# Last attention pair: where the embedding average and the first experts' preparation stand in the instruction order

## The reference

```python
h = tok(x)                                # patches @ W + b + pos, class token in front
h = concatenate([h, txt], axis=1)         # 178 tokens
h = h + attn(layernorm(h))
h = h + ffn(layernorm(h))

# attn: 12 heads, causal
xn  = layernorm(x, ln_w)
avg = mean(wte, axis=0)                   # wte is 50257 x 192
Q   = xn * W_qk[head]
a   = softmax(causal(Q @ Q.T / sqrt(192)))
out = a @ (xn - avg)                      # per head
out = out / [1 .. S]                      # per row
out = concat(heads) @ W_o.T

# ffn: 16 routed experts and a shared one, hidden size 128
s = softmax(x @ gate_w + gate_b)          # 4 of 8 groups, then 4 of 16 experts, weights times 2.5
y = sum over experts of w * (silu(x @ Wu + bu) * (x @ Wg + bg)) @ Wd + w @ bd
y = y + shared expert
```

## Time and profile before

| what | value |
|---|---|
| median of 3 runs | 476.73 us (476.62 to 477.12) |
| profiled execution, its own time | 476.07 us |
| its span | 474.2 us |
| PE busy | 448.3 us (95%) |
| DVE busy | 279.2 us (59%) |
| ACT busy | 181.8 us (38%) |
| mean granted TensorE clock | 0.977 of full |

### The profile page before, as it was taken

One profiled execution on the slowest core, in us unless ns is written; L12 is line 12 of the kernel. 1 busy time (PEld: TensorE's weight loads), 2 busy tenths in 40 slices (PEclk: granted clock), 3 DMA queues, 4 the chain that ended last, 5 costly groups with the idle time before them and its releaser, 6 DMA issues. The chain is left out here.

```text
span 474.2 us, 7663 instructions
## 1 busy us (share of the span) xinstructions
PE 448.3 (95%) x2836; PEld 403.3 (85%) x2836; DVE 279.2 (59%) x789; ACT 181.8 (38%) x581; POOL 97.5 (21%) x110
## 2 busy tenths in 40 slices
PE   8699999999999999982998999989999999999997
PEld 7488779877898778972866999989999999999996
DVE  4488866476654976304497635697447654754443
ACT  1467566256644376411445035532312232121211
POOL 3012122221122211210013015921180027000000
PEclk9799999999999999996799999999999999999999
DMA  8968999999999999978316022322323222222220
GB/s 208 252 242 155 212 214 213 213 214 214 213 213 215 212 214 214 212 138 200 133 38 238 1 74 67 64 47 65 86 63 64 63 85 59 60 73 72 75 65 25
DMA packets 23686, 65.01 MB, mean 137 GB/s; under 512 B 2876, under 2 KB 13332, under 8 KB 23266
## 3 DMA queue, kind: packets, MB, share of 16 engines
q0 software_dynamic: 7904, 40.86, 41.1%
q1 hardware_dynamic: 14882, 22.68, 17.9%
q10 hardware_dynamic: 864, 1.00, 0.7%
HBM read 61.88 MB, written 1.27 MB: 133 GB/s over the span
## 5 line engine op out<-in xcount | busy, mean ns | idle before, releaser
L805 PE MATMUL bank<-woT,area_o 128*128 128x192 f32 (+1 forms) x432 | 71.9, 327 | 0.0
L520 ACT ACTIVATE pm<-bank,nmax 128x128 f32<-128x128 f32 x96 | 34.5, 369 | 96.2 <-DVE nmax L1024 96.2
L1110 DVE TENSOR_TENSOR area_b<-area_b,area_w 128x356 f32<-128x356 f32 x64 | 33.9, 529 | 62.7 <-ACT area_b L585 62.6
L805 PEld LDWEIGHTS bank<-woT,area_o 128*128 128x128 f32 (+1 forms) x432 | 69.8, 182 | 0.6 <-issue 0.6
L422 POOL DMA_DIRECT2D area_w<-in_L_attn_wte_dram x26 | 31.4, 1226 | 127.7 <-DMA area_w<-in_L_attn_wte_dram 127.7
L887 PE MATMUL bank<-area_w_r,area_o_r 128*128 128x356 f32 x112 | 43.9, 392 | 0.0
L585 ACT ACTIVATE area_b<-bank,area_k 128x356 f32<-128x356 f32 x32 | 17.8, 558 | 58.9 <-PE bank L891 58.9
L754 PE MATMUL bank<-pT,xn 128*128 128x356 f32 x96 | 39.7, 495 | 0.0
L543 ACT ACTIVATE area_b<-xb,w 64x192 f32<-64x192 f32 x96 | 38.3, 447 | 0.8
L923 PE MATMUL bank<-area_k,area_b 128*128 128x192 f32 (+1 forms) x192 | 36.8, 327 | 0.0
L888 PE MATMUL bank<-area_w_r,area_o_r 128*128 128x356 f32 x112 | 36.4, 325 | 0.0
(11 more groups left out here) (218 smaller groups left out, 1019.4 us busy)
## 6 DMA issues: line engine op xcount, KB each, us to landing
area_w<-in_L_attn_wte_dram POOLq DMA_DIRECT2D x28, 1344.0 KB, 12.6
area_w<-gate_rows SPq DMA_DIRECT2D x64, 178.0 KB, 3.0
area_k<-in_experts_dram SPq DMA_DIRECT2D x8, 353.0 KB, 6.5
area_a<-in_experts_dram SPq DMA_DIRECT2D x6, 353.0 KB, 5.1
woT<-in_L_attn_W_o_dram SPq DMA_DIRECT2D x1, 1728.0 KB, 15.9
area_o<-in_x_dram SPq DMA_DIRECT2D x4, 384.0 KB, 9.1
area_w<-area_w POOLq DMA_DIRECT2D x1, 1344.0 KB, 9.8
area_b<-in_experts_dram SPq DMA_DIRECT2D x3, 353.0 KB, 6.4
```

The costliest lines, as they stand in the source:

```text
L520: act.activation(pm[:, sl, n, :], SIDE[k][:, j * P:(j + 1) * P], ACT.Exp, bias=nmax[:, sl, n:n + 1], accum_out=psums[:, sl, n:n + 1])
L805: last = pe.matmul(o, oT[:, c, at:at + n], woT[:, c, :], start=(c == 0), stop=(c == NCH - 1))
L1110: dve.tensor_tensor(sil[:, n % 2, :], sil[:, n % 2, :], wbc[:, m % RING, :], ALU.mult).then_inc(weighted, 1)
```

## The change

In the last pair, the wait for the fold and DVE's additions go from loop step 0 to step 3, and `mean`, the copy of `avg` and `mean_projected` to step 4. `correct(0)` goes behind step 5's copies of the turned probabilities, `experts_in(0)` behind the last unit's `mix_out`, and `correct(1)` behind `w_stack(1)`. PE now has the last projection cut in pieces: 12 matmuls of tile 0, `turn_a(0)`, the other 6, `turn_b(0)`, 5 matmuls of tile 1, `gate(0)`, the other 13, tile 2, and then `turn_rows(0)`. On ACT, `w_high(0)` goes one step later, and `features_a(0)`, `features_b(0)` and `w_high(1)` go behind the pair. The same instructions are issued in both kernels, but for where a group is split.

```diff
@@ ACT
-                    if u == 3 and last:
+                    if u == 4 and last:
                         w_high(0)
-                    if u == 4 and last:
-                        features_a(0)
-                        w_high(1)
...
                 prob_out(5, U + 5)
-                if last:
-                    features_b(0)
...
+            features_a(0)
+            features_b(0)
+            w_high(1)
             w_high(2)
@@ PE
-                    if u == 1 and last:
+                    if u == 4 and last:
                         mean()
-                    if u == 2 and last:
-                        mean_projected()
                     turn_probs(u, U + u)
                     if u == 4 and last:
-                        turn_a(0)
+                        mean_projected()
...
                 turn_probs(5, U + 5)
-                if last:
-                    turn_b(0)
...
                 mix(5, U + 5, i)
                 if last:
                     pe.wait_ge(s_small2, 80)
+                    project(i, 0, 0, 12)
+                    turn_a(0)
+                    project(i, 0, 12, NCH)
+                    turn_b(0)
+                    project(i, 1, 0, 5)
                     gate(0)
-                project(i, 0)
-                project(i, 1)
-                if last:
+                    project(i, 1, 5, NCH)
+                    project(i, 2)
                     turn_rows(0)
-                    project(i, 2)
+                else:
+                    project(i, 0)
+                    project(i, 1)
@@ DVE
+                    if u == 4 and last:
+                        dve.wait_ge(avg_psum, 1)
+                        dve.tensor_copy(avg[:], bank[7][:, 0:2]).then_inc(avg_ready, 1)
...
                     if last:
-                        if u == 0:
+                        if u == 3:
                             part = wacc[:, 0]
                             dve.wait_ge(wte_fold, 16)
...
-                        if u == 1:
-                            dve.wait_ge(avg_psum, 1)
-                            dve.tensor_copy(avg[:], bank[7][:, 0:2]).then_inc(avg_ready, 1)
-                        if u == 2:
-                            dve.wait_ge(c_psum, 1)
-                            link(dve.tensor_copy(cbc[:], bank[7][:, E:2 * E]))
-                            correct(0)
-                        if u == 3:
-                            experts_in(0)
-                        if u == 4:
-                            correct(1)
...
                 tails_out(5, U + 5)
...
+                else:
+                    dve.wait_ge(c_psum, 1)
+                    link(dve.tensor_copy(cbc[:], bank[7][:, E:2 * E]))
+                    correct(0)
                 mix_out(5, U + 5)
...
                 else:
+                    experts_in(0)
                     w_stack(0)
                     w_stack(1)
+                    correct(1)
                     logits(0)
```

More of the change, by code:

```diff
@@ L788, in turn_rows, with project @@
                 last.then_inc(wT_psum, 1)
-            def project(i, t):
+            def project(i, t, first=0, end=NCH):
                 at, n = COLS[t]
-                if t == 0:
+                if t == 0 and first == 0:
                     pe.wait_ge(ot_act, UPP * i + UPB)
@@ L799, in project @@
                         pe.wait_ge(xnT_ready, 4 * i + 8)
-                if t == 1:
+                if t == 1 and first == 0:
                     pe.wait_ge(ot_act, UPP * (i + 1))
@@ L803, in project @@
                 o = projected(i, t)
-                for c in range(NCH):
+                for c in range(first, end):
                     last = pe.matmul(o, oT[:, c, at:at + n], woT[:, c, :], start=(c == 0), stop=(c == NCH - 1))
-                last.then_inc(wo_done, 1)
+                if end == NCH:
+                    last.then_inc(wo_done, 1)
             turn_in(0, 0, 0)
```

## The result

The changed kernel takes 462.06 us (median of 4 runs, 460.75 to 462.67), the kernel before 476.68 us (476.04 to 477.12): a ratio of 0.969, 95% interval 0.966 to 0.972, or 14.6 us less. The forecast was 461.0 us. The profiled execution is the fastest of the four, 460.75 us with a span of 458.8 us, against 460.3 us in the sum.

The account below looks back on a forecast made before the run. PE, busy 95% of the span, was taken as the bound, so the first expert's start decides: 277.61 to 261.9, 15.7 us off 476.07 gives 460.3 us profiled, 461.0 us median; forecast 459.5 to 462.5 (0.70), range 459.3 to 465.5.

Parts of the forecast that it names:

- (a): PE's 9.93 us stop before `mean`: goes, since PE's next work is the turning of unit 1, from 212.19.
- (b): Units 1, 2 and 3 on PE at full clock: 6.28 us each, 18.84 us together.
- Rivals 3 and 5: Fold lands later (a 20 us fold: about 465 us), chance 0.04; wait returns elsewhere in full, change does nothing, 0.01.
- (c): `mean` ahead of unit 4's turning: 2.0 us at full clock, bounds 2.02 and 2.95, no wait for the fold.
- (d): Unit 4's turning up to the last mixing on PE: last mixing starts at 239.46, 16.5 us earlier than before.
- (e): Last mixing to first expert: 22.45 us with 0.2 us wait before `turn_rows`; first expert at 261.9, 15.7 us earlier.
- (f): Gate weights' broadcast reads behind `turn_rows`: land 5.2 us into the experts, hidden with 0.6 us to spare.
- Rival 1: The chain to `wts` or the broadcast is late: 462.5 to 465.5 us, chance 0.16.
- The half clock: PE work behind the stop at half clock: about 4.0 us of the last mixing's 16.5 us, 2.0 in `mean`.
- rival 2: Clock falls all the same from something that remains; units 2 and 3 lose 6 us: about 467 us, chance 0.04.
- Rival 4: Short idle gaps hold the clock at half from unit 4's turning to the first expert: 490 us, slower, chance 0.03.
- The forecast's sign of being wrong: PE stopping over 1.5 us before `turn_rows` or second `down`, clock 0.50 anywhere over 212 to 262, or waiting before `mean`.

Follow-up runs that it names:

- late_fold: Changed kernel with nine small POOL operations ahead of the folding DMA, to make it land later: 462.86 us, ratio 0.972.
- logits_first: Changed kernel with `correct(1)` moved behind the choice of the experts and `turn_rows` 4 matmuls ahead of the projection's end: 461.58 us, ratio 0.968.
- unsplit: Changed kernel with the last projection whole again, both transposes and the gate ahead of it: 471.07 us, ratio 0.989.
- awake: Kernel before the change, with 28 matmuls that nobody reads ahead of PE's wait for the additions: 476.06 us, ratio 1.000.
- small_fold: Kernel before the change, with the folding DMA cut to one of its 14 rows per partition so it lands early: 467.65 us, ratio 0.983.
- spread: Changed kernel with `mean`'s three groups of ten records set apart and `mean_projected` between last turning and last mixing: 460.89 us, ratio 0.967.
- both: Changed kernel with the edits of `spread` and `logits_first` together: 459.75 us, ratio 0.965.

## Why the prediction held, and which term was mis-sized

**The stop (a) and the units (b).** Right. PE's 9.93 us are gone and three units take 6.28 us each. The fold landed 1.4 us later than before (221.10 against 219.71), well inside the slack, and `late_fold` shows that 7.0 of 7.4 us of further delay cost nothing. Rivals 3 and 5 are out. The turning of unit 1 began at 211.79 where I had 212.19; of these 0.40 us 0.23 were there already at the pair's first turning (205.51 against 205.74), which nothing in the change explains, and which is luck.

**The average (c).** 2.18 us at full clock where I took 2.02 and bounded it by 2.95.

**The last mixing (d) and the projection (e).** The last mixing started at 239.25 (forecast 239.46), the first expert 22.89 us later (forecast 22.45), with 0.30 us of idle time in front of `turn_rows` (forecast 0.2). `logits_first` shows what made that wait: `correct(1)` ahead of the logits. It took 3.12 us there (250.70 to 253.82) where I had 2.5, because its first three operations (L1083) took 1.75 us, against 1.08 in the kernel before (L1082); why, the trace does not say. `unsplit` shows what the pieces of the projection hide: 4.96 us of idle time, and behind it some 4 us of half clock that I had not counted as being at stake. The profiled execution came out at 460.75 us against a sum of 460.3, and part of that closeness is errors that cancel: 0.40 us too late at the start, then 0.16 too little for `mean` and 0.44 too little for the last stretch.

**The broadcast (f).** Late by 1.04 us on DVE, absorbed before PE, as forecast. Rival 1 is out.

**The half clock.** This is the mis-sized term. I counted 4.0 us for it as part of the 16.5, because I took the stop to be its only cause, and I gave a fall of the clock in the changed kernel little chance (rivals 2 and 4), since it had stood at 1.00 beside short gaps. There are two causes. The stop lowers the clock (it fell at 216.5 with PE idle, and stayed at 1.00 when `awake` filled the stop). And the clock also falls straight behind `mean` with PE busy and no stop ahead: in `unsplit`, `logits_first` and one of the changed kernel's two profiles, though not in the other and not in `late_fold`. (In `small_fold` and `awake` a rest of the stop stood ahead of `mean`, and the two cannot be told apart.) Moving `mean` does not take that away. In the changed kernel it happens in a part of the executions, at 1.6 us each, so that of the 4.0 us only about 2.4 come back there. That is most of the distance between the median, 462.06, and the forecast, 461.0: the two runs at a clock of 0.993, 460.75 and 461.48, lie around the forecast, the other two 1.7 us above it. The forecast's sign of being wrong, a clock of 0.50 anywhere in 212 to 262, so did appear, in the changed kernel's second profile but not in its first, and rival 2 was right in its kind: something that remains lowers the clock. It put the loss at 6 us, and it is 1.6. Rival 4 looked to idle gaps and a clock that stays at half up to the first expert; neither is there.

`spread` points to `mean` in one piece as the cause: with the same instructions ten at a time none of three profiles (`spread`, `both` and the one behind it) has the fall, and the median is 1.6 us lower. It is not closed, since only three of five profiles with `mean` whole and no stop had the fall, and one run of `both` had a low clock. That the fall in the remaining runs, for which only clocks are known, is the same one, is argued from their clocks (0.988 and 0.989 with it in profiles, 0.991 to 0.993 without), not shown; a run of `late_fold` with 0.987 took 462.17 us, 1.4 us less than two with 0.989, so a low mean clock alone does not tell where it was low or what it cost. The rest of the spread may come from the low clock of the start, which begins at 14.5 to 17.7 us, differently from one execution to the next; that is not shown.

The Trainium skill's rule (page "TensorE: Matmul & The Clock Gate", section "What's actually happening") is that the gate is set by how busy PE has been of late. The traces agree for the stop. Behind `mean` PE's busy time as the profile shows it, 5.00 of 5.00 us and then 3.00 of 3.00 at a clock of 0.50 (`unsplit`), would by that rule speak for a full clock; the trace does not agree, and the measurement decides.

## What to carry to other kernels

A wait of PE can cost its own length and then, as here, some 8 us of work at half clock, so a term of the sum that comes from a clock must ask for each cause of its fall: fill the stop with matmuls that nobody reads once, and see whether the clock holds. Moving work away from a late input paid in full here as long as the new place is behind the landing, and the slack can be measured by making the input later still. When one matmul stream is cut to hide a chain of other engines, put each link where the chain has arrived, and look at what queues in front of the chain's next link on the other engine: here `correct(1)`, which nobody needed yet.

## What the runs showed of the hardware that was not expected

- A run of 30 matmul records of one moving column (2.2 us, back to back, PE shown as busy 2.30 of 2.30 us) was followed within 0.5 to 1.3 us by a granted clock of 0.50 for 3.4 us, the 1.2 GHz level, with no idle time, in three of five profiles. Ten such records at a time, among larger matmuls, were not, in three profiles.
- How long PE stood does not by itself order the cases. In `small_fold` a stop of 2.75 us and `mean` behind it left the clock at 1.00 for 2.0 us more, and it fell at 217.0. In `unsplit` a stop of 3.12 us, followed by small transposes and a gap of 0.92 us, had the clock fall in that gap, and 10.2 us at 0.50 followed. At the start of the kernel with both edits PE stood for 2.07 us up to 14.31, did small transposes, and stood for 1.05 us from 15.2 on; the clock fell at 15.7.
- The accumulating DMA of 1344 KB within the chip's SBUF took 9.7 to 11.4 us in ten profiles: 9.8 us once with every engine but DMA idle (before) and once with all of them at work (`late_fold`), 10.7 to 11.4 us in the other eight; what sets it stays open.
- The half clock at the start of the kernel (6.8 us at 0.50, from between 14.5 and 17.7 on) is in the profile of every kernel but the last, where ten more matmuls that nobody reads removed it.
